# A fourth weight slot, gates of 512 columns, a shorter routing and 90 identity turns in a transformer layer on one core

## The reference

```python
x = _layernorm(x + attention(x))
scores = sigmoid(x @ gate_w.T) + expert_bias           # 16 experts in 4 groups
# the 2 groups with the best maximum, and in them the 4 best experts
w = original_scores[idx]; w = w / sum(w)
h = silu(x @ w1[e]) * (x @ w3[e])                      # 512 -> 352, each expert
y = sum over the 4 picked experts of w * (h @ w2[e])   # 352 -> 512
z = silu(x @ sw1) * (x @ sw3) @ sw2                    # two shared experts, all tokens
x = _layernorm(x + y + z)
```

## Time and profile before

| | |
|---|---|
| time, median of 3 runs | 2453.92 us (2452.63 to 2455.18) |
| profiled execution | 2429.61 us, span 2427.8 us, mean granted clock 0.951 |
| PE busy | 2228.2 us (92%) |
| POOL busy | 1341.3 us (55%) |
| DVE, ACT busy | 1408.0 us (58%), 1167.3 us (48%) |
| attention ends, `front` begins | 1508.1 us |
| `routed` begins on PE | 1735.2 us |
| `combine` begins on PE | 2316.5 us |

### The profile page before, as it was taken

The page is one execution under the profiler, slowest core; times in us unless marked ns, Lnnn a source line. Parts: engine busy times, 40 slices in busy tenths (PEclk is TensorE's granted clock), DMA queues, the critical chain, the costliest instruction groups (busy, mean ns, idle before and its releaser), DMA issues. The chain is left out here.

```text
span 2427.8 us, 45003 instructions
## 1 busy us (share of the span) xinstructions
PE 2228.2 (92%) x13203; PEld 2005.4 (83%) x13204; DVE 1408.0 (58%) x4707; ACT 1167.3 (48%) x3712; POOL 1341.3 (55%) x1934
## 2 busy tenths in 40 slices
PE   6899999999999999999999996989999999878863
PEld 4789998998998998998999995867799998768752
DVE  5677776676666676766767776282223323443256
ACT  2556666665665665665666665421233333333221
POOL 2776666666666665765666764437501103473376
PEclk8999999999999999999999999589999999989986
DMA  4400600000000000000000001214523324564256
GB/s 140 195 21 21 272 10 22 16 7 22 19 4 22 19 4 23 19 4 23 19 4 21 1 1 42 74 37 187 192 81 112 113 78 151 172 196 144 98 162 184
DMA packets 68600, 177.79 MB, mean 73 GB/s; under 512 B 11584, under 2 KB 15232, under 8 KB 68224
## 3 DMA queue, kind: packets, MB, share of 16 engines
q1 hardware_dynamic: 37184, 87.15, 10.9%
q0 software_dynamic: 18928, 67.01, 8.5%
q10 hardware_dynamic: 12240, 20.73, 2.3%
HBM read 107.74 MB, written 67.13 MB: 72 GB/s over the span
## 5 line engine op out<-in xcount | busy, mean ns | idle before, releaser
L771 POOL TENSOR_TENSOR cross<-nat,rope_tables 128x128 f32<-128x128 f32 x256 | 150.5, 588 | 431.0 <-DVE nat L633 431.0
L926 PE MATMUL bank<-whi,xT_lo 128*128 128x384 f32 x1024 | 371.0, 362 | 3.1 <-PEq L177 2.0
L927 PE MATMUL bank<-wlo,xT_hi 128*128 128x384 f32 x1024 | 348.7, 341 | 0.0
L928 PE MATMUL bank<-whi,xT_hi 128*128 128x384 f32 x1024 | 348.4, 340 | 0.0
L1480 POOL TENSOR_TENSOR ring_lo<-staged,ring_hi 128x1088 fp32r<-128x1088 f32 x48 | 121.1, 2537 | 405.1 <-ACT ring_hi L1442 401.0
L592 DVE TENSOR_TENSOR acc<-acc,bank 128x512 f32<-128x512 f32 x256 | 176.0, 687 | 229.3 <-PE bank L928 213.0
L705 ACT COPY probT<-bank 128x128 f32<-128x128 f32 (+3 forms) x256 | 109.4, 427 | 382.6 <-PE bank L542 382.5
L926 PE MATMUL bank<-ring_hi,xslo 128*128 128x352 f32 x600 | 205.6, 343 | 27.8 <-issue 26.4
L714 ACT ACTIVATE prob<-prob,nbias,rstd 128x256 f32<-128x256 f32 (+1 forms) x256 | 152.5, 596 | 103.4 <-DVE nbias L620 93.8
L926 PEld LDWEIGHTS bank<-whi,xT_lo 128*128 128x128 f32 x1024 | 196.3, 192 | 3.8 <-issue 2.2
L928 PE MATMUL bank<-ring_hi,xshi 128*128 128x352 f32 x600 | 197.0, 328 | 0.0
(11 more groups left out here) (290 smaller groups left out, 6286.8 us busy)
## 6 DMA issues: line engine op xcount, KB each, us to landing
staged<-in_wexp POOLq DMA_DIRECT2D x60, 544.0 KB, 5.0
slots_in<-zeros SPq DMA_DIRECT2D x41, 512.0 KB, 6.0
xslot<-slots_in SPq DMA_DIRECT2D x76, 256.0 KB, 2.6
slots_out<-yslot ACTq DMA_DIRECT2D x76, 256.0 KB, 2.0
wraw<-in_wh SPq DMA_DIRECT2D x16, 768.0 KB, 4.2
staged<-in_wexp SPq DMA_DIRECT2D x20, 544.0 KB, 3.8
slots_out<-zeros SPq DMA_DIRECT2D x9, 512.0 KB, 6.3
acc<-in_x SPq DMA_DIRECT2D x4, 1024.0 KB, 12.0
```

The source lines that it names most:

```text
L771: pool.tensor_tensor(cross[:, :, :], nat[:, a.two, :, 0:2 * ROT], sin, ALU.mult).then_inc(s_mult, 1)
L926: pe.matmul(out, wl_, xh_, start=first, stop=False)
L927: pe.matmul(out, wh_, xl_, start=False, stop=False)
L928: return pe.matmul(out, wh_, xh_, start=False, stop=last)
```

## The change

`RING` becomes 4 and there is one staging buffer only. Ahead of expert e's tiles, ACT casts quarters 0 and 1 and DVE quarters 2 and 3 of expert e + 2 (of experts 1 and 2 ahead of expert 0). POOL makes all four low parts of each expert, and behind each the DMA of the same quarter of the next one. The last shared expert is prepared in the same way. In `front` the gates go by chunk: the gate weights are the stationary operand (16 columns) and 512 tokens move, so the logits come out as 16x512; DVE copies them and PE turns them back (`logits_back`). Two gate turns stand ahead of the wait for `g_in`. The picks come from `dve.max` with running sums for ties in place of the 16-step rank; the counts are 32 matmuls in place of two and stand behind `down(0, 1)`; weights and tile tables are worked out later, in chunk 1; POOL makes 3 of the hidden blocks, not 6; `add_shared` reads the banks, without ACT's copies. `combine` has 4 gather buffers instead of 6. And PE turns the identity 90 times at the end of `heads`.

```diff
-RING = 3
+RING = 4
@@ heads
             pe_pair(pe, NP - 1, last=True)
+            for _ in range(90):
+                pe.transpose(b_score[0][:, 0:P], ident[:, :], ident[:, :])
@@ front
-    POOL_BLOCKS = NB
+    POOL_BLOCKS = 3
-                def gate_logits(n):
-                    pe.wait_ge(s_raw, n + 1)
-                    for k in range(KC):
-                        mm = pe.matmul(b_logits[:, n * E:(n + 1) * E], raw[:, n % RAWS, k * P:(k + 1) * P], gateT[:, k, :],
-                                       start=(k == 0), stop=(k == KC - 1))
-                    mm.then_inc(s_gl, 1)
+                def gate_logits(i):
+                    c, k = divmod(i, KC)
+                    if k == 0:
+                        wait_for(pe, s_lgc, c - 1)
+                    pe.wait_ge(s_raw, i + 1)
+                    pe.matmul(bank[2 + c % 2][0:E, :], gateT[:, k, :], raw[:, i % RAWS, :],
+                              start=(k == 0), stop=(k == KC - 1)).then_inc(s_gl, 1)
+                def counts():
+                    pe.wait_ge(s_pick, 1)
+                    picks = pickedb[:, :, :].rearrange("p n e -> p (n e)")
+                    pe.matmul(b_count, trib[:, 0, :], picks, start=True, stop=False)
+                    for m in range(1, NT):
+                        pe.matmul(b_count[:, m * E:NT * E], trib[:, 1, :], picks[:, 0:(NT - m) * E], start=False,
+                                  stop=(m == NT - 1))
+                    for m in range(NT):
+                        mm = pe.matmul(b_load, trib[:, 1, :], picks[:, m * E:(m + 1) * E], start=(m == 0),
+                                       stop=(m == NT - 1))
+                    mm.then_inc(s_count, 1)
+                for i in range(2):
+                    gate_turn(i)
                 pe.wait_ge(g_in, 64)
...
-                        if c == 0 and q == 3:
...
+                        if c == 0 and q == 2:
+                            counts()
...
+                for n in range(NT):
+                    count[0] += 1
+                    dve.max(best[:, n, :], choice[:, n, :]).then_inc(s_r, 1)
...
+                def add_shared(c):
+                    dve.wait_ge(s_scat[c], 16 * TPC * PICK)
@@ routed
-        staged = [staged_first, sb("staged1", [P, WCOLS], F32, st)]
+        AHEAD = 2
+        def prepared_at(e):
+            return range(1, AHEAD + 1) if e == 0 else range(e + AHEAD, e + AHEAD + 1)
...
+            for q in qs:
+                staged_in(eng, f, q)
+                copy(whi[:, f % RING, quarter(q)], staged[:, quarter(q)]).then_inc(s_hi, 1)
...
-                for e in range(1, E + 1):
...
+                for f in range(1, LAST + 1):
+                    for q in range(QUARTERS):
+                        done = (f - 1) * QUARTERS + q + 1
+                        if q < 2:
+                            pool.wait_ge(s_hi_act, (f - 1) * 2 + q + 1)
+                        else:
+                            pool.wait_ge(s_hi_dve, (f - 1) * 2 + q - 1)
+                        pool.tensor_tensor(wlo[:, f % RING, quarter(q)], staged[:, quarter(q)],
+                                           whi[:, f % RING, quarter(q)].bitcast(F32), ALU.subtract).then_inc(s_w, 1)
+                        if f < LAST:
+                            pool.wait_ge(s_w, done)
+                            pool.dma_start(staged[:, quarter(q)], t["wexp"][f + 1, :, quarter(q)]).then_inc(st_in[q], 16)
...
-                    wait_for(pe, s_w, e * (QUARTERS - 1))
-                    wait_for(pe, s_w_dve, e)
+                    wait_for(pe, s_w, e * QUARTERS)
@@ combine
-        NG = 6
+        NG = 4
```

More of the change, by code:

```diff
@@ L1268, in _ @@
                 then(dve.tensor_copy(trib[:, :, :], tri))
+                for x_ in (*runs, *tiles):
+                    zeroed_ = x_[:, :, :] if len(x_.shape) == 3 else x_[:, :]
+                    then(dve.memset(zeroed_, 0.0))
+                then(dve.tensor_scalar(texp[:, 0:E], ramp[:, 0:E], float(P), None, ALU.mult))
+                for c in range(NCH):
+                    dve.wait_ge(s_gl, (c + 1) * KC)
+                    wait_for(dve, s_gb, c)
+                    dve.tensor_copy(logitT[:, :], bank[2 + c % 2][0:E, :]).then_inc(s_lgc, 1)
+                x_low(0, 0)
+                x_low(0, 1)
                 dve.wait_ge(s_sig, 1)
@@ L1320, in _ @@
-                dve.wait_ge(s_count, 1)
-                ne = lambda b: b[:, :, :]
-                within, sums = (bank[0][:, x * NT * E:(x + 1) * NT * E].rearrange("p (n e) -> p n e", e=E) for x in range(2))
-                then(dve.tensor_copy(before[0][:, :, :], sums))
-                full = prefix(before, NT, ne)
-                then(dve.tensor_copy(load[:, :], full[:, NT - 1, :]))
-                then(dve.tensor_tensor(full[:, :, :], full[:, :, :], sums, ALU.subtract))
-                then(dve.tensor_tensor(full[:, :, :], full[:, :, :], within, ALU.add))
@@ new lines, in _ @@
+                dve.wait_ge(s_r, count[0])
+                limit = best[:, :, PICK - 1:PICK].to_broadcast([P, NT, E])
+                ties, run1, run2 = runs
+                then(dve.tensor_tensor(cmp[:, :, :], choice[:, :, :], limit, ALU.is_gt))
+                then(dve.tensor_tensor(by_tile(ties, 0), choice[:, :, :], limit, ALU.is_equal))
+                then(dve.tensor_reduce(csum[:, :], cmp[:, :, :], AX.X, ALU.add))
+                then(dve.tensor_scalar(csum[:, :], csum[:, :], -1.0, float(PICK), ALU.mult, ALU.add))
@@ new lines, in _ @@
+                place = by_tile(running(ties, [run1, run2], by_tile), 0)
+                then(dve.tensor_tensor(place, place, picked, ALU.mult))
+                dve.wait_ge(s_count, 1)
+                within = b_count.rearrange("p (n e) -> p n e", e=E)
+                then(dve.tensor_tensor(by16[:, :, :], b_load.unsqueeze(2).to_broadcast([P, E, E]),
+                                       texp[:, 0:E].unsqueeze(1).to_broadcast([P, E, E]), ALU.is_gt))
+                then(dve.tensor_reduce(load[:, :], by16[:, :, :], AX.X, ALU.add))
```

365 lines of the change are left out of this document (158 added, 207 removed).

## The result

The changed kernel takes 2476.70 us in the median (2474.86 to 2478.92, 4 runs), the kernel before in the same comparison 2454.55 (2452.63 to 2455.56, 4 runs): ratio 1.0111, 95% interval 1.0058 to 1.0165. It is 22 us (1.1%) slower. The prediction said 2453.6, within 2444 to 2476.

A forecast was written before the change was run, and what follows sets the result against it. TensorE was taken as the bound: gates by its instructions at half clock, routed experts with gaps. Front −18, routed start +16, one-tile experts +10.7, end −9 sum to −0.3: 2453.6 us, range 2444 to 2476.

The forecast's parts named there:

- The scale: Whole kernel: profiled time 2429.61 us, median of runs 2453.92; the difference of 24.3 us is added to the forecast.
- Turns: End of PE's heads block: 90 turns take 9.9 us at full clock and give nothing back; +5.5 us.
- Rival 2: End of heads: the 90 turns fall to half clock, gates probably cold too; +28, 2482 us; chance 0.07.
- Gates: Gates: 16 steps of 1.33 us, clock rising after some 4 us, 24 us instead of 39.5; −15.5 us.
- rival 1: Gates stay at 1.2 GHz: −15.5 becomes +3 and the −2 goes; +20, 2474 us; chance 0.25.
- The −2 at the first ups: First up matmuls behind the gates: half of some 4 us at half clock is spared; −2 us.
- Routing: Picks and counts: PE's wait for picks 3 us instead of 10.8, 1 for the clock, −9; counts +2.7 us.
- The 0 for the scatter's earlier start: Front: the 64 transfers start earlier, beside the next chunks' ups; DVE's new wait for the scatter costs 0.
- Start of routed: Before the first down matmul: PE waits for casts of experts 1 and 2, 12.5 us late, 3 for clock; +16.
- One-tile experts: Routed: four stalls at experts with one tile, 11.5 us instead of 7.7, +15; experts behind them −4.3; together +10.7.
- End: End of routed: last expert prepared with expert 15, block ends at 2302.7 instead of 2311.2; −9 us.
- rivals 3 and 4: Routed: 3, no wait for staging, likelier 2446 us; 4, ring neutral at one-tile experts, −11; chance together 0.18.

The follow-up runs named there:

- The second trace: The kernel before with no edit, profiled and timed again: 2463.10 us (2439.04 to 2471.72, 10 runs), span 2469.9.
- the wait every 4: POOL waits behind every 4 scatter transfers instead of 16: changed kernel 2453.90 us, kernel before 2457.95, kernel before with changed front and no turns 2414.32.
- without the scatter: The 64 indirect scatter transfers replaced by one plain write per chunk: changed kernel 2453.32 us, kernel before 2432.72.
- front only: The kernel before with the changed front, without the 90 turns, routed and combine as before: 2437.59 us, ratio 0.9946.

## Why the prediction was wrong, step by step

*The scale.* I added 24.3 us, the difference of profile and median, as if it were a constant of the kernel. The second trace puts it in the waits beside the scatter, which the profiled execution happened not to have. The changed kernel has as many in its usual runs (2476.7 against 2453.3 without), so the step did no harm here, which is luck; the reason was wrong, and with the wait every 4 it would have been off by 23 us.

*Turns*: +5.5 predicted, 5.4 measured, at full clock to the last; with the gates' later rise of the clock they cost 6.2. Rival 2 is out, and with it, for these turns over 10 us, the rule of the Trainium skill's page "TensorE: Matmul & The Clock Gate", Part 4, that I had named.

*Gates*: −15.5 predicted, −12.3 measured. The clock rose, after 5.7 us and not 4, within 4 in the kernel without the turns (rival 1 is out). A step at full clock is 1.55 us and not 1.33: a pair of matmuls takes 0.97. The −2 at the first ups did not come: PE waited 3.29 us ahead of them and began them at half clock.

*Routing*: the step "Wait 0 to 6, I take 3 with 1 for the clock: −9" was too small: the wait was 7.67, since one operation of DVE was held to 6.23 us, and the row with 4.008 had shown no longer hold. In the kernel without the turns POOL's low parts came behind the picks, and the wait was 0.52. −2.9 came of the −6.3 that I had with the counts (170.5 to 167.6, both without the scatter). The 0 for the scatter's earlier start holds: with all 64 transfers and the wait every 4 the stretch is 167.7 us.

*Start of routed*: +16 predicted. From ACT's cast of expert 0 to that of expert 1 the changed kernel takes 122.4 us against 105.4: +17.0. The chain was the predicted one: four low parts, the fetch behind the last, DVE's cast, shlo. Its wait of 14.85 was larger than the 12.5 that I had, by the longer set and by DVE's casts held to 3.15.

*One-tile experts*: +10.7 predicted, +25 measured (70.0 us over tiles times 6.69, from expert 5 on, against 44.9). **This is the failed step**, in the words: "In the expert behind it GpSimd's period of 12.3 a set is absorbed better, 2.7 three times". The four big ones were near: 11.0, 10.9, 7.6 and 10.9 us of wait with the slow clock behind them, 49.4 in all where I had 46. But the expert behind each had 5.6, 4.5, 4.9 and 2.6 to bear, 17.6 in all, where I had 2.7 three times, 8.1. And the 12.3 that I took off for these experts before was not there: they took 1.4, 1.3, 1.4 and 1.3, and the four big ones 37.0 and not 4 times 7.7. So a term of −4.3 was +12.3, and the four big ones were +12.5 where I had +15. One set is 4 times 3.38 = 13.5 us on POOL, not 12.3, since it waits for its own low part and then issues, and two sets in a row push each other: with one staging buffer the next set's quarters are fetched only as this one's are read. Before, the second buffer held them already. That what is late in one expert is made good in the next was carried over from a kernel with two buffers. That the one buffer decides the sum is argued and not shown. One expert ahead (67.4 us at the one-tile experts), the second expert in another place (68.8) and a shorter set on POOL (69.2) all kept the 68.9, though the last moved it from the experts behind to the big ones, and the old stage with two buffers (44.9) does not have it. But the old stage differs in more than the buffer, and a ring of four with two staging buffers was not tried.

*End*: −9 predicted, −7.5 measured. *Combine*: 0 predicted, 0.3 measured.

In sum, without the waits beside the scatter, the profiled executions have spans of 2453.5 and 2429.2 us: +24.3, of which 2.2 are attention in these two executions. Against the predicted −0.3 the routed stage took 14 us more (31.5 in this pair, 34.4 with the scatter, 17.7 predicted), the gates with the first ups 5, the picks and counts 3. Rival 1 gave 2474, nearly the time, for a cause that the trace excludes; rivals 3 and 4 are out with the waits of 76 us. The front's terms add to −18.3, which I had written as −18. The 4.9 us that I took for what a measurement can tell is too little as well, with runs of one kernel over 33 us.

## What to carry to other kernels

Profile a kernel twice before taking one trace's stage lengths as its own: a difference between profile and median can be a part of the kernel, and should be found before a change is priced. When a buffer is taken away from a pipeline, price two of the short rounds in a row, not one: what a round could make good, it could through that buffer. And what stands ahead of an operation that PE waits for, on VectorE beside GpSimd, is priced held (3 us for 0.7), not free.

## What the runs showed of the hardware

Long lines of indirect transfers went with late completion signals of TensorE. With 16 in line, signals came 6 us and more after the records' end, and PE waited 14 to 28.5 us in four traces (both kernels, without the turns and front only among them) and not at all in a fifth, of the kernel before. With 8 in line it was 2.3 us, with 4 none, in three kernels. What joins the two is open: at one place the trace shows the semaphore event and the end of POOL's wait together (1619.93 and 1620.17), at others (1632.42) a late start in the middle of a group, and no reason. No run changed the number of engines or the size of a transfer.

Ninety turns of 0.11 us with nothing else on TensorE kept the granted clock at 1.00 for 10 us, and turns mixed with matmuls of 512 columns brought it from 0.50 to 1.00 in 5.7 us, and within 3.8 in the kernel without the turns.

An operation of VectorE that takes 0.42 us elsewhere took 6.23 beside three GpSimd operations in a row, so the hold was not limited to one of them.
